# Cross-attention on one core: the first batch's shift in two halves, the outputs two batches behind, K's rounding on ScalarE

## What is computed

```python
Q = (query @ Wq.T + bq)          # 8 x 112 x 256, split into 16 heads
K = (key_value @ Wk.T + bk)      # 8 x 375 x 256
V = (key_value @ Wv.T + bv)
scores = einsum('bhqd,bhkd->bhqk', Q, K) / sqrt(16)
attn = softmax(scores, axis=-1)
context = einsum('bhqk,bhkd->bhqd', attn, V)
x = context @ W_o.T + b_o + query
out = (x - mean(x)) / sqrt(var(x) + 1e-5) * ln_gamma + ln_beta
```

## Time and profile before

| | us |
|---|---|
| median of 3 runs | 155.61 (154.75 to 156.13) |
| the profiled run, device time | 157.02 |
| its span, first to last instruction | 155.2 |
| mean granted TensorE clock in the span | 0.982 of 2.4 GHz |

### The profile page before, as it was taken

The page is one execution under the profiler, slowest core; times in us unless marked ns, Lnnn a source line. Parts: engine busy times, 40 slices in busy tenths (PEclk is TensorE's granted clock), DMA queues, the critical chain, the costliest instruction groups (busy, mean ns, idle before and its releaser), DMA issues.

```text
span 155.2 us, 3853 instructions
## 1 busy us (share of the span) xinstructions
PE 134.0 (86%) x1466; PEld 116.7 (75%) x1466; DVE 105.6 (68%) x247; ACT 80.4 (52%) x163; POOL 60.7 (39%) x83
## 2 busy tenths in 40 slices
PE   5799989679979999889998998999899996779850
PEld 4599779468768899769988987899787875667620
DVE  6745997757937769947896699578779887031252
ACT  3648437214426666526655666465656565566410
POOL 8946997920003998404140504130023023041051
PEclk9999999987999999999999999999999999999997
DMA  4976989698950250697414050405031001001002
GB/s 128 358 259 216 269 296 227 159 270 239 301 204 2 102 156 0 169 267 235 135 52 151 4 178 4 155 2 183 24 128 34 4 4 30 4 4 30 4 0 59
DMA packets 14354, 19.58 MB, mean 126 GB/s; under 512 B 2192, under 2 KB 13520, under 8 KB 14336
## 3 DMA queue, kind: packets, MB, share of 16 engines
q1 hardware_dynamic: 13056, 17.26, 35.6%
q0 software_dynamic: 592, 1.70, 4.5%
q10 hardware_dynamic: 688, 0.38, 0.8%
HBM read 6.30 MB, written 0.92 MB: 47 GB/s over the span
## 4 chain that ended last, share of the span: by engine, by line
PE 65%; DVE 11%; DMA 10%; ACT 6%; issue 5%; SPq 1%; POOLq 0%; ACTq 0%; DVEq 0%
PE m_bank L793 19%; PE pv_bank L873 12%; PE st_bank L857 11%; PE mx_bank L834 10%; DMA q_stack<-shift 6%; DVE mx L656 6%; PE m_bank L901 4%; DMA c_raw<-ctxT 3%; PE m_bank L884 2%; ACT pw L561 2%; PE st_bank L793 2%; DMA q_stack<-q_first 1%; DVE q_hl L618 1%; PE m_bank L841 1%; ACT o_normT L552 1%
## 5 line engine op out<-in xcount | busy, mean ns | idle before, releaser
L656 DVE TENSOR_REDUCE mx<-mx_bank 112x1 f32<-112x375 f32 x128 | 64.6, 541 | 20.4 <-PE mx_bank L834 19.8
L561 ACT ACTIVATE pw<-st_bank 125x448 f32<-125x448 f32 x90 | 48.5, 548 | 48.5 <-PE st_bank L857 47.7
L834 PE MATMUL mx_bank<-k_stack,q_stack 128*112 128x376 f32 x128 | 41.3, 351 | 2.2 <-DVE mx L656 1.2
L857 PE MATMUL st_bank<-q_stack,k_stack 128*125 128x224 f32 x180 | 37.7, 294 | 1.7 <-DMA q_stack<-shift 1.7
L857 PEld LDWEIGHTS st_bank<-q_stack,k_stack 128*125 128x125 f32 x180 | 30.0, 190 | 5.5 <-issue 3.0
L834 PEld LDWEIGHTS mx_bank<-k_stack,q_stack 128*112 128x112 f32 x128 | 22.0, 181 | 4.5 <-DVE mx L656 2.4
L359 POOL TENSOR_TENSOR c_hl<-c_raw,c_hl 128x752 fp32r<-128x752 f32 x6 | 10.9, 1814 | 27.5 <-DVE c_hl L612 27.5
L873 PE MATMUL pv_bank<-pw,v_sb 125*17 125x112 f32 x720 | 20.4, 260 | 1.1 <-ACT o_raw L535 1.1
L405 POOL TENSOR_SCALAR var_eps<-mv 112x1 f32<-112x1 f32 x7 | 1.6, 223 | 49.2 <-DVE mv L692 49.2
L793 PE MATMUL m_bank<-c_hl,w_hl 128*128 128x376 f32 x84 | 18.7, 365 | 0.9 <-ACT w_hl L449 0.9
L873 PEld LDWEIGHTS pv_bank<-pw,v_sb 125*17 125x17 f32 x720 | 16.3, 97 | 3.9 <-issue 2.2
(11 more groups left out here) (102 smaller groups left out, 160.6 us busy)
## 6 DMA issues: line engine op xcount, KB each, us to landing
k_stack<-k_hl SPq DMA_DIRECT2D x48, 188.0 KB, 2.5
c_raw<-ctxT SPq DMA_DIRECT2D x8, 375.0 KB, 4.3
q_stack<-q_hl SPq DMA_DIRECT2D x6, 224.0 KB, 4.5
q_stack<-q_hl SPq DMA_DIRECT2D x6, 168.0 KB, 3.4
x_space<-x_nat POOLq DMA_DIRECT2D x1, 896.0 KB, 10.3
out<-yo SPq DMA_DIRECT2D x8, 112.0 KB, 1.9
pw<-wT SPq DMA_DIRECT2D x2, 256.0 KB, 4.8
x_space<-xT SPq DMA_DIRECT2D x1, 448.0 KB, 6.1
```

What stands on the lines that cost most here:

```text
L561: nc.scalar.activation(p_tile[0:KC, n % PR, :, :], st_of(n)[0:KC, 0:4 * Q].rearrange("p (j q) -> p j q", j=4), ACT.Exp, scale=float(DK) ** ...
L656: nc.vector.tensor_reduce(mx[b % 2][:, h % 2, q_pair(h // 2):q_pair(h // 2) + 1], mx_bank[n % MR][0:Q, 0:KV], axis=AX_X, op=ALU.max, negat ...
L834: nc.tensor.matmul(mx_bank[n % MR][0:Q, 0:KVP], q_stack[k][:, side, q_pair(h // 2), b - Q_STACKS[k][0], :], k_stack[b % 3][:, h // 2, :], ...
L857: last = nc.tensor.matmul(st_of(n)[0:KC, k * 2 * Q:(k + 1) * 2 * Q], k_stack[i % 3][:, 2 * g + k, c * KC:(c + 1) * KC], q_stack[qk][:, :, ...
```

## The change

It rewrites the order of the loop and moves some operations to other engines. What is computed stays the same.

- **First shift in halves.** The maxima of heads 0 to 7 of batch 0 are rounded, transposed (behind head 9), copied and written by two DMAs of their own; those of heads 8 to 15 follow in units 0 and 1 of batch 0. Units 0 to 5 need the first half only. 14 heads instead of 20 stand before the loop; V and Q of batch 2 move into units 1 to 5, K of batch 3 into units 6 and 8, V of batch 3 and the transposition for batch 1 into unit 11. The identity matrix is made earlier on GpSimd, the clearing of a K stack later.
- **Outputs later.** OT is in unit 8, ONT goes into the bank of the shift's transposition one batch later (`NORM_WITH`), OUT is in unit 2 two batches later still: output 0 in batch 3, 1 in 4, and 2, 3 and 4 in batch 5, 5 in batch 6, 6 in batch 7. The bias of V moves from batch 0 to batch 1.
- **K on ScalarE.** From batch 3 on ScalarE copies K from PSUM to `k_full` and rounds it in a second pass (`take_k`); the remainder is a subtraction on GpSimd (`subtract_k`) in place of VectorE's. The bank is free after the first pass. The rounding of the later contexts moves from VectorE to ScalarE. `scale_to_norm` moves from VectorE to GpSimd.
- **Maxima and shifts.** 20 heads in batch 0, 23 in batch 1, then 16 in each, so that they still end in unit 4 of batch 6; the rounding is in unit 5 and the transposition in unit 6 (it was in 7), its DMA after exponential 7 (it was 9).

The diff, cut:

```diff
-U_K = (0, 2)
-U_V = (3, 5, 8)
-U_OT, U_ONT, U_OUT = 5, 9, 11
-U_BIAS = 4
-U_Q = (5, 10)
-U_NEGATE, U_MT, U_SHIFT = 5, 7, 9
-U_CONTEXT = 7
-HEADS = (1, 1, 2, 1, 2, 1, 1, 1, 2, 1, 2, 1)
-EARLY_HEADS = H + 4
-EARLY_JOBS = {1: ("Q", 1, 0), 3: ("Q", 1, 1), 5: ("V", 1, 0), 7: ("V", 1, 1), 9: ("V", 1, 2), 11: ("K", 2, 0),
-              13: ("K", 2, 1), 14: ("V", 2, 0), 15: ("V", 2, 1)}
+U_OUT, U_OT, U_BIAS = 2, 8, 1
+U_K = (3, 5)
+U_V = ((11, 11, 11), (10, 11, 11), (9, 10, 11))
+NORM_WITH = {3: 0, 4: 1, 5: 2, 6: 4, 7: 5}
+U_MT = (11, 9, 6, 6, 6, 6, 6)
+U_NEGATE = (10, 8, 5, 5, 5, 5, 5)
+EARLY_HEADS = 14
+EARLY_JOBS = {1: ("Q", 1, 0), 3: ("Q", 1, 1), 5: ("V", 1, 0), 7: ("V", 1, 1), 9: ("MT", 0, 0), 10: ("V", 1, 2),
+              11: ("K", 2, 0), 13: ("K", 2, 1)}
+FIRST_JOBS = {1: (("MT", 0, 1), ("V", 2, 0)), 2: (("V", 2, 1),), 3: (("V", 2, 2),), 4: (("Q", 2, 0),), 5: (("Q", 2, 1),)}
+FIRST_K = (6, 8)
...
+    (M1_JOBS if _i == 0 else M0_JOBS).append(("MT", _i + 1))
+    M0_JOBS.append(("V", _i + AHEAD, 0))
+    M1_JOBS.append(("V", _i + AHEAD, 1))
...
-FIRST_HEADS = (2, 3, 2, 3, 2)
+HEADS = (2, 1, 1, 1, 2, 1, 1, 1, 2, 1, 2, 1)
+FIRST_HEADS = ((2, 1, 2, 2, 2, 2, 2, 2, 2, 1, 1, 1), (2, 2, 2, 2, 2, 2, 2, 1, 2, 2, 2, 2))
...
-            "K": lambda b, t: (k_lo, 2 * b + t + 1),
+            "K": lambda b, t: (k_lo, 2 * b + t + 1) if b < AHEAD else (k_taken, 2 * (b - AHEAD) + t + 1),
-            "MT": lambda b: (shift_ready, b + 1),
+            "MT": lambda b, *half: ((o_normT_ready, NORM_WITH[b] + 1) if b in NORM_WITH else
+                                    (shift_ready, half[0] + 1 if b == 0 else b + 2)),
...
-                if i >= 2:
-                    store(i - 2)
+                if 3 <= i <= 5:
+                    store(i - 3)
...
+            def subtract_k(b, t):
+                pool.wait_ge(k_hi, 2 * b + t + 1)
+                nc.gpsimd.tensor_tensor(k_hl[b % 2][:, 1, t, :], k_full[:, t, :], k_hl[b % 2][:, 0, t, :].bitcast(F32),
+                                        op=ALU.subtract).then_inc(k_lo, 1)
...
-                nc.gpsimd.tensor_tensor(yo[b % 2][:, :], z[b % 2][:, :], g_rows[:, :],
+                nc.gpsimd.tensor_scalar(yo[b % 2][:, :], z[b % 2][:, :], mv[b % 2][:, 0:1], rstd[:, 0:1],
+                                        op0=ALU.subtract, op1=ALU.mult).then_inc(y_ready, 1)
+                pool.wait_ge(y_ready, b + 1)
+                nc.gpsimd.tensor_tensor(yo[b % 2][:, :], yo[b % 2][:, :], g_rows[:, :],
                                         op=ALU.mult).then_inc(y_scaled, 1)
...
-            for i in range(B + 2):
-                if i >= 2:
-                    inverse_deviation(i - 2)
-                if 2 <= i < B + 1:
-                    scale_rows(i - 2)
+            for i in range(B):
+                if 3 <= i <= 5:
+                    inverse_deviation(i - 3)
+                    scale_rows(i - 3)
                 if i + AHEAD + 1 < B:
                     context_lo(i + AHEAD + 1)
                 if i == 0:
+                    clear_q()
+                if i == 1:
                     bias_into_x()
-                    clear_q()
+                if i + AHEAD < B:
+                    for t in range(2):
+                        subtract_k(i + AHEAD, t)
+            for b in range(3, B - 1):
+                inverse_deviation(b)
+                scale_rows(b)
+            inverse_deviation(B - 1)
...
+            def take_k(b, t):
+                src = wait_full(act, "K", b, t)
+                if b > AHEAD:
+                    act.wait_ge(k_lo, 2 * (b - 1) + t + 1)
+                nc.scalar.activation(k_full[:, t, :], src[:, 0:KVP], ACT.Identity,
+                                     bias=bqk[:, 2 + t:3 + t]).then_inc(k_taken, 1)
+                act.wait_ge(k_taken, 2 * (b - AHEAD) + t + 1)
+                act.wait_ge(k_in[(b - 2) % 3][t], 48 * ((b - 2) // 3 + 1))
+                nc.scalar.copy(k_hl[b % 2][:, 0, t, :], k_full[:, t, :]).then_inc(k_hi, 1)
...
-            for n in range(2):
-                v_part(1, n)
+            v_part(1, 0)
             x_hi_part(2)
-            context_hi(3)
-            for t in range(2):
-                k_hi_part(2, t)
-            v_part(2, 0)
+            def stack_shift_half(t):
+                act.wait_ge(shift_ready, t + 1)
+                for side in range(2):
+                    act.dma_start(q_stack[0][SPREAD - 1:2 * SPREAD:SPREAD, side, t:NP:2, 0, :].bitcast(F32),
+                                  shift_half[t][NP * side:NP * (side + 1), :].bitcast(F32)).then_inc(half_in[t], 16)
-            stack_shift(0)
-            v_part(2, 1)
+            stack_shift_half(0)
+            v_part(1, 1)
+            context_hi(3)
+            for t in range(2):
+                k_hi_part(2, t)
             act.wait_ge(w_lo, 2)
...
+                    if u == 1 and i == 0:
+                        stack_shift_half(1)
+                    if u in (2, 3) and i == 0:
+                        v_part(2, u - 2)
+                    if u in (4, 5) and i == 0:
+                        q_hi_part(2, u - 4)
+                    if u == (1 if i < B - 1 else 3) and i >= 1:
+                        context_hi(i + AHEAD + 1)
+                    if u in (FIRST_K if i == 0 else U_K) and i + AHEAD < B:
+                        take_k(i + AHEAD, (FIRST_K if i == 0 else U_K).index(u))
+                    if i + 1 < B and u == min(U_MT[i] + 1, UNITS - 1):
                         stack_shift(i + 1)
-                    if u == (2 if i < B - 1 else 4) and i >= 1:
-                    if u - 1 == U_ONT and i >= 1:
-                        take_o_norm_t(i - 1)
-                    if u - 1 in U_V[1:] and i + AHEAD < B:
-                        v_part(i + AHEAD, U_V[1:].index(u - 1))
-                    if u - 1 in U_Q and i == 0:
-                        q_hi_part(2, U_Q.index(u - 1))
+                        if i + 1 in NORM_WITH:
+                            take_o_norm_t(NORM_WITH[i + 1], "MT", i + 1)
+                    if u == 5 and i == 5:
...
+            def negate_half(t):
...
-            negate(0)
-            take_shift(0)
-            for t in range(2):
-                k_lo_part(2, t)
-            for n in range(H, EARLY_HEADS):
-                head_max(n)
+                if n == H // 2 - 1:
+                    negate_half(0)
+                if n == H // 2 + 1:
+                    take_shift_half(0)
+                if n == 12:
+                    k_lo_part(2, 0)
...
+                    if u == 0 and i == 0:
+                        k_lo_part(2, 1)
+                    if u == 1 and i == 0:
+                        take_shift_half(1)
+                    if u in (5, 6) and i == 0:
+                        q_lo_part(2, u - 5)
+                    if u == 0 and i == 1:
+                        take_bv()
+                    if u == U_BIAS and i == 1:
+                        bias_rows()
+                    if u == U_OUT and 3 <= i <= 5:
+                        layer_norm(i - 3)
+                    if i + 1 < B and u == U_NEGATE[i]:
+                        negate(i + 1)
+                    if i + 1 < B and u == U_MT[i]:
+                        take_shift(i + 1)
+                    if u == U_OT and 1 <= i <= 4:
                         normalise(i - 1)
-                    if u == U_NEGATE and i + 1 < B:
-                        negate(i + 1)
+                    if u == 4 and i in (5, 6):
+                        normalise(i - 1)
+                    if u == 5 and i == B - 1:
+                        normalise(B - 2)
+                    if u == 7 and i == 5:
+                        layer_norm(3)
+                    if u == 10 and i in (5, 6):
+                        layer_norm(i - 1)
                     if u == 5 and i == B - 2:
                         nc.vector.memset(mx_bank[2][:, :], 0.0).then_inc(pv_clear, 1)
+                    if u == 0 and i == 0:
+                        negate_half(1)
...
-                dst, full = claim("ONT", b)
+            def norm_columns(dst, b):
                 pe.wait_ge(o_norm_ready, b + 1)
...
-            pe.wait_ge(ident_ready, 1)
-            transpose_max(0)
-            v_project(2, 2)
-            for n in range(H, EARLY_HEADS):
-                scores_for_max(n)
-            for n in range(2):
-                pe.wait_ge(v_ready, 2 * 2 + n + 1)
+            pe.wait_ge(v_ready, 4)
...
+                    if i == 0:
+                        for kind, *at in FIRST_JOBS.get(u, ()):
+                            projects[kind](*at)
+                    if u == U_BIAS and i == 1:
+                        bias_of_values()
+                    if u == U_OUT and 3 <= i <= 5:
+                        out_project(i - 3)
+                    if u == U_OT and 1 <= i <= 4:
                         transpose_o(i - 1)
-                    if u == U_BIAS and i == 0:
-                        bias_of_values()
-                    if u in U_Q and i == 0:
```

(19 more changed lines are left out.)

202 lines of the change are left out of this document (103 added, 99 removed).

## The result

The changed kernel is slower: 162.13 us, median of 4 runs (160.05 to 163.97), against 155.69 (154.75 to 156.13) of the kernel before; the ratio is 1.034 with an interval of 1.022 to 1.045. The forecast was 150.3 us. The profiled execution has a span of 160.8 us at a mean granted clock of 0.946; before it was 155.2 at 0.982. Times of one kernel scatter here by 1 to 4%, and only in part with the clock that TensorE was granted, so each ratio in this text is taken over comparable runs on one chip and can differ from that of the medians (1.041 here).

What follows compares the result with a forecast made beforehand. TensorE was taken to bound batches 1 to 4, VectorE nearly batch 5, chains batches 6, 7 and the end. Stage terms summed to 149.9 against 155.2 us; 5.3 less than the 155.6 median gave 150.3, range 147.0 to 153.6.

Steps and rivals of the forecast that it cites:

- only the two small operations of `negate` are exposed, so the sum stays: Work moved to GpSimd: its mutual exclusion with VectorE touches only the rounding's two small operations, so no time was added.
- Start, 28.9: Stage before batch 0: first shifted score at 28.9 us instead of 32.9, second DMA issued at 25.3 plus 3.7 us landing.
- Both bounds of that step: First shift's landing: 29.6 us if each DMA issue takes 1.24 us, 27.3 us if it lands 1.99 us after issue.
- Batch 0: Batch 0: 19.0 to 20.2 us, plus a 1.2 us stall before batch 1; 1.7 us of lower-clock loss kept.
- the third rival: Batch 0 starts 4 us earlier but ends as now, in ScalarE's order; total within 1%, about 155 us; chance 0.10.
- Batch 1, 15.3: Batch 1: 15.9 to 15.3 us, seven more heads and the bias against the projection and waits taken away.
- Batch 2, 13.3: Batch 2: 14.85 to 13.3 us, less 0.74 for no output projection and 0.8 for its wait.
- Batch 5, 13.2: Batch 5: 11.2 to 13.2 us, two more layer norms of 1.0 us each on a full VectorE.
- Batch 6: Batch 6: 11.9 to 10.3 us; 1.05 us wait for `o_normT` goes, 0.6 of layer norm leaves, 1.2 us stall stays.
- Slower: the lower clock: Rival: 1.2 GHz held through batches 0 and 1 costs 15.8 us, 166 in all; decides from 14 us on; chance 0.07.
- Only a small gain: Rival: slower DMA issue, 2.6 us stall before batch 1, 1.2 us idling per added batch 5 projection; 153.6 us; chance 0.11.
- Halts of 1.0 to 1.3 us later in the trace left the clock at 1.00: Argument against the lower-clock rival, from the earlier trace's later halts of TensorE; that rival's chance was 0.07.

Runs made afterwards that it cites:

- e15_after: The changed kernel run again beside other runs on one chip: 161.89 us (158.19 to 164.61; kernel before there 157.2).
- e10_spread_xb_lock: `e9_spread_xb` with GpSimd also waiting for the first `neg_half` before it subtracts x of the third group: 158.61 us, ratio 1.010 (1.002 to 1.018).
- e7_spread: Changed kernel with the bias addition in batch 2, output 2 in batch 4 and output 4 in batch 6: 159.03 us, ratio 1.018 (1.007 to 1.029).
- e3_bias_late: Changed kernel with GpSimd's bias addition to x in batch 2, behind its K subtractions, not in batch 1: 158.66 to 174.61 us, no ratio.
- e9_spread_xb: `e7_spread` with the transfer of `x_nat` moved behind `clear_q` in batch 0: 157.8 us, ratio 1.000 (0.986 to 1.014).
- e1_fill: Changed kernel with unread 64-column matmuls (44, 14, 16, 24) in four halts of TensorE: 166.71 us, ratio 1.072 (1.060 to 1.084).
- e5_dense: Changed kernel with fewer unread matmuls of 512 columns (14, 5, 5, 8) in the same four halts: 162.54 us, ratio 1.046 (1.034 to 1.058).
- e12_kdve: Changed kernel with K split as before, high part on ScalarE and remainder on VectorE out of PSUM: 164.68 us, ratio 1.049 (1.040 to 1.058).
- e6_before_dense: Kernel before with unread 512-column matmuls, 3 before head 17 and 4 before batch 0: 155.86 us, ratio 0.998 (0.994 to 1.003).
- e2_before_fill: Kernel before with 32 unread 64-column matmuls before batch 0: 161.2 us, ratio 1.039 (1.029 to 1.049).
- e4_out_early: Changed kernel with output projection and layer norm of batch 2 in unit 10 of batch 4, not in batch 5: ratio 1.036 (1.017 to 1.054).

## Why the prediction was wrong, by its steps

Between the forecast span and the measured one lie 11 us. The largest part is batch 1, where the step "only the two small operations of `negate` are exposed, so the sum stays" put the collision with GpSimd at nothing; then batch 5, which was priced on VectorE; then the start. In both batches a stretch at 1.2 GHz came on top, for which the sum had no term.

**Start, 28.9: mis-sized by up to 1.75.** The half was ready at 24.6 us, as forecast. Both DMAs were issued by 26.5; the second was issued 0.6 us later than forecast, and the step "with the same 3.7 us, lands at 28.9" gave 4.60 us in the first profile, 4.12 in `e15_after`, where the score came at 28.90, and 4.63 in `e10_spread_xb_lock`. Both bounds of that step lay under 30.65. The 28.90 is luck: one and the same early halt of TensorE, 0.56 us before a maximum, begins at 21.92 us in the kernel before, at 22.15 in the first profile and at 20.90 in `e15_after`, with the same work ahead of it. Counted from there the first score came 2.5 and 3.0 us sooner than in the kernel before, not 4.

**Batch 0: length right by luck.** 21.5 against 21.4. Its waits were shorter than forecast, 1.08 us for the second half's rounding instead of 1.6 and 0.46 before batch 1 instead of 1.2, and the stretch at 1.2 GHz was twice as long, 6.8 us instead of 3.4. `e15_after` has 23.49 and `e7_spread` 23.72, since the second half's shift took 7.87 us in `e7_spread` and 8.97 in `e15_after`, where unit 6 waits 1.63 us. The forecast looked at one landing and left out what the second one travels with; of that only `x_nat` was tested. Batch 1 at 52 is the third rival's outcome, but not by the order of ScalarE's work that it named.

**Batch 1, 15.3: the largest miss, in three parts.** At full clock and without the halt it takes 17.05 (`e3_bias_late`), 1.75 over. TensorE's busy time rose by 1.7 us over the earlier trace rows, not by the 1.0 of the step, and its idle time fell only from 1.3 to 0.7 us, where the step took away 1.6, more than there was. Then the halt, 1.3 us: the step quoted above named the cause and priced it at nothing because the operations are small. What was paid is what was left of GpSimd's instructions, and what waits is TensorE. Then the clock, 1.5.

**Batch 2, 13.3: a wait took the place of another.** 14.1: TensorE waits 0.58 us for ScalarE's `k_full` at the transposition of the output. The text had called a wait ended by ScalarE in batches 2 to 4 a sign that it was wrong, as it had a clock below 0.85 in batch 0, which was 0.84. **Batches 3 and 4:** right, 14.14 and 14.11 for 14.15.

**Batch 5, 13.2: priced on the wrong engine.** The step held VectorE to be full. It was busy for 10.68 of 14.72 us in `e15_after`. TensorE's busy time rose from 10.88 to 12.52 (two projections), and it idled 2.2 us where the earlier trace rows has 0.35, 1.9 of it on the rounding, which stands on VectorE behind a layer norm and `normalise` and for which the transposition of the output now waits too; 0.45 of it is GpSimd's again. 3.5 us at full clock instead of 2.0, and 1.6 more with the stretch in the first profile. **Batch 6:** 0.9 gained of 1.6. The wait for `o_normT` went and the stall of 1.2 us stayed, at 1.14, both as forecast; new are 0.68 us of waiting for a maximum, which stands on VectorE behind the last layer norm of batch 5.

**The rivals.** "Slower: the lower clock", with 0.07, has the right outcome and half of the cause. It was to decide from 14 us at 1.2 GHz on, and there were 13.6; but the two added stretches cost 3.1 us, and without them the changed kernel would still not be faster. A slowdown with the clock as it was stood in no rival. "Only a small gain" counted its 1.2 us in batch 5 once, though it gave it to each of two projections. "Halts of 1.0 to 1.3 us later in the trace left the clock at 1.00" was true of the kernel before, and no ground for the changed one. In batch 1 the link is close: both profiles of the changed kernel have the halt (64.55 and 64.8 us) and the stretch (from 68.4 and 67.3); `e3_bias_late`, `e7_spread`, `e9_spread_xb` and `e10_spread_xb_lock` have neither, nor have `e1_fill` and `e5_dense` the stretch, where the halt was filled. In batch 5 it isn't: the halt of 1.9 us is in the first profile, in `e15_after`, `e3_bias_late` and `e12_kdve`, and only the first has a stretch behind it, while `e1_fill` has the stretch with the halt filled. In `e6_before_dense` the clock fell in batch 6, where in the kernel before the same halts left it at 1.00. A halt is thus no sure cause and its absence no sure protection. Which halts do so in general stays open.

## What to carry to other kernels

A wait that is removed uncovers what landed behind it, so ask of each what else became ready during it: here the shift's DMA stood behind `o_normT`, and the second half behind the first. Before work goes to GpSimd, look where its instructions fall against VectorE's small SBUF operations that TensorE waits for; the price is up to the length of GpSimd's instruction, whatever VectorE's own. Where the total of halts changes, carry a term for the granted clock in both directions, and read a gain in one batch together with the batch that receives the moved work.

## What was not expected of the hardware

- A stretch at 1.2 GHz lasted with TensorE recorded as fully busy: 34.0 to 44.0 us of `e2_before_fill`, during and behind 32 matmuls of 64 columns that took 6.9 us. Matmuls of 512 columns in the same place left batch 0 of `e6_before_dense` at 1.00.
- VectorE's operation on 112 x 8 numbers took 1.74 us although its record starts 0.09 us ahead of GpSimd's, and ended within 0.04 us of it. A `tensor_scalar` of GpSimd on 112 x 256 took 1.23 us where a `tensor_tensor` took 0.73; the forecast had 0.73 to 1.0.
- Transfers of the same half shift took from 3.03 to 8.97 us, by what else was under way.
- The execution of `e4_out_early` that took 312 us has a granted clock of 1.00 throughout, yet its maxima scores took 697 ns each on average, where those of the changed kernel took 361. No run here shows why.
